# Inverse attention denominators: broadcast by DMA through DRAM instead of by matmul, and denominators in four column groups

## The chip, the cores and the metric

One Trainium2 chip; the same program runs on its 8 cores, each on its own share of the data (4 of 32 sequences), with no traffic between cores. The metric is the device time in microseconds of the slowest core. A core has TensorE (PE, matmuls), VectorE (DVE), ScalarE (ACT), GpSimd (POOL), SyncE (SP, which here issues nearly all DMAs, in order) and 16 DMA engines.

## The reference

For x of shape (32, 2048, 1024), one transformer layer with linear attention (16 heads of 64) and a quantized feed-forward net:

```
Qf, Kf = relu(heads(LN(x) Wq') P) + 1e-6, relu(heads(LN(x) Wk') P) + 1e-6
KV    = sum over tokens of Kf^T V          (per sequence and head, 64x64)
Ksum  = sum over tokens of Kf              (per sequence and head, 64)
denom = Qf . Ksum + 1e-6                   (per token and head)
out   = (Qf KV) / denom
x     = x + LN(out Wo' + bo)
h     = round(256 (LN(x) w1 + b1)) / 256;  h = piecewise-linear GELU(h), rounded
x     = x + LN(round(256 (h w2 + b2)) / 256)
```

## The kernel before

Everything lies in one straight-line program. `p.T`, `p.V`, `p.S`, `p.G` and `p.dma("Y", ...)` append an instruction to the list of TensorE, VectorE, ScalarE, GpSimd and SyncE, with the tokens it waits for; each engine runs its own list strictly in the order in which the Python code appended it. So the order of the calls is the schedule, and a DMA that waits on SyncE holds every later DMA of SyncE.

Phase 1 (`for t in range(NT)`, 64 tiles of 128 tokens, 16 per sequence): layer norm, DMA transpose into `xnT`, projections to K features, V and Q features, and the accumulation of KV and Ksum. Q features go to DRAM (`qscr`), four tiles at a time, with a lag of three tiles. At each sequence's end `kv_mask` makes `ksz[s]`, the Ksum vector spread over a 128 x 8 x 16 matrix that is zero except where column = head, and `m_chunk` folds KV with Wo into `mscr` in DRAM. `k_const` makes the constants `chs` that complete the denominators.

Phase 2 (`for g in range(NBLK * NQ + LAG)`, 32 blocks of 256 tokens, 8 slots i = 0..7 each): in slot (j, i) TensorE does the slot's eighth of the feed-forward net of block j (`ff_w1`, 32 matmuls of 256 columns, and `ff_w2`, 16 matmuls of 512 columns for the slot three before), and between them the "front" of the next block J = j + 1: `fr_den` (denominators), `fr_bc` and `fr_qn` (normalising the Q features `qf`), `fr_o` (attention output by `msb`, twice 16 matmuls), then `fr_sq`, `fr_x2`, `fr_sq2`, `fr_xn` and a DMA transpose into `xnF` for the next block's `ff_w1`. The "fi_" steps end the block before (drain, layer norm, residual, store).

Before the change block J's denominators are one group of 8 matmuls onto 16 PSUM partitions (slot 0, L538); VectorE adds `chs`, takes the reciprocal and splits it into two bf16 halves `hilo` (L541 to L547); in slot 1 eight matmuls with the 0/1 matrix `sel` spread the 16 rows over the 128 partitions of each chunk (`fr_bc`, L554), and `fr_qn` (L564) multiplies `qf` by what stands in PSUM. Block 0's front and the last six Q chunks (`last_q`) stand between the two phases (L870 to L925). The edges of the phases' order that matter:

```
        kv_acc(NT - 1); kv_out(s); last_q(2); fr_den(0); last_q(3)
        for k in range(2): fr_bc(0, k); fr_qn(0, k)
        last_q(4)
        ...
        o_seed(0, 0); fr_o(0, 0); fr_sq(0, 0); kv_mask(s); last_q(6)
```

## Time and profile before

| | |
|---|---|
| times of three runs | 3126.4, 2863.38, 3311.34 us (median 3126.4) |
| the profiled execution's own time | 2864.24 us |
| its span (core 3, the slowest) | 2862.7 us, cores 2856.7 to 2862.7 us |
| mean granted TensorE clock of that core | 0.994 |
| PE, DVE, ACT, POOL busy | 98%, 72%, 64%, 16% |
| mean DMA rate | 171 GB/s |

The span is the time from the first to the last instruction of a core; the profiled execution's own time is 1.5 us more than its span. The profile was taken with the granted clock near full on every core, and its time agrees with the lowest of the three runs. "Idle before" is time in which an engine had nothing under way, with what released it. PE busy is a modelled number: a matmul's record lasts about 160 ns longer than its turn in a stream, so costs of matmuls in a stream are read from the distance between starts.

### The profile page before, as it was taken

What the parts mean: (1) busy time and instruction counts of PE and PEld (TensorE: products, weight loads), DVE (VectorE), ACT (ScalarE), POOL (GpSimd) and SP (SyncE); (2) the same over time, 40 slices, a digit from 0 to 9 for tenths busy, and PEclk for the clock granted to TensorE, in tenths of its full rate; (3) what the DMA queues carried; (4) which work ended last, traced back from release to release, by engine and by line L of the source; (5) the groups of instructions that cost most, each with busy time, mean ns of one, the idle gap of its engine ahead of it and who ended that gap; (6) DMA issues with size and microseconds to landing.
All of it is one profiled execution on the core that took longest, in us unless ns stands there. A gap on an engine that the chain in (4) does not pass through costs nothing.

```text
span 2862.7 us, 47693 instructions; the slowest of 8 cores (2856.7 to 2862.7 us)
## 1 busy us (share of the span) xinstructions
PE 2801.9 (98%) x17762; PEld 1704.7 (60%) x17762; DVE 2063.2 (72%) x2657; ACT 1846.1 (64%) x2953; POOL 467.6 (16%) x1092
## 2 busy tenths in 40 slices
PE   6999999999889999999999999999999999999998
PEld 3444444444456666666666666666666666666665
DVE  5454344443378888788888888788888888878887
ACT  3222222222377787878777787878777788878776
POOL 0111111110001111211111111211111112212111
PEclk8999999999999999999999999999999999999999
DMA  8547999853445555565666556556665655555654
GB/s 261 137 102 130 156 146 160 157 125 85 150 142 177 177 177 174 178 196 184 189 193 182 177 177 197 178 174 182 185 201 180 198 185 163 178 177 179 192 181 147
DMA packets 287618, 488.91 MB, mean 171 GB/s; under 512 B 141424, under 2 KB 174320, under 8 KB 287392
## 3 DMA queue, kind: packets, MB, share of 16 engines
q1 hardware_dynamic: 278176, 469.08, 55.9%
q0 software_dynamic: 9216, 16.78, 5.2%
q8 instruction: 147, 2.41, 0.3%
q14 instruction: 79, 0.65, 0.1%
HBM read 412.90 MB, written 67.11 MB: 168 GB/s over the span
## 4 chain that ended last, share of the span: by engine, by line
PE 96%; DMA 1%; DVE 1%; ACT 1%; issue 0%; POOL 0%; SPq 0%; POOLq 0%; DVEq 0%; ACTq 0%
PE bk L668 31%; PE bk L726 30%; PE bk L371 8%; PE bk L585 8%; PE bk L389 8%; PE bk L402 7%; PE bk L538 1%; PE bk L421 1%; PE bk L554 1%; DMA wkf<-wk_n 1%; PE bk L479 0%; DMA qf<-qscr 0%; PE bk L311 0%; DMA xnF<-xn 0%; ACT stq L226 0%
## 5 line engine op out<-in xcount | busy, mean ns | idle before, releaser
L668 PE MATMUL bk<-xnF,w 128*128 128x256 bf16 x8192 | 937.2, 273 | 4.5 <-DMA xnF<-xn 1.3
L726 PE MATMUL bk<-w2r,yb 128*128 128x512 bf16 x4096 | 925.6, 379 | 0.0
L668 PEld LDWEIGHTS bk<-xnF,w 128*128 128x128 bf16 x8192 | 801.6, 98 | 146.5 <-issue 6.7
L681 ACT ACTIVATE kbuf<-bk,b1s 128x256 int32<-128x256 f32 x1024 | 426.5, 472 | 413.0 <-PE bk L668 413.0
L726 PEld LDWEIGHTS bk<-w2r,yb 128*128 128x128 bf16 x4096 | 398.3, 98 | 441.8 <-issue 6.5
L703 DVE TENSOR_TENSOR y1b<-y1b,y0b 128x1024 f32<-128x1024 f32 x256 | 312.4, 1220 | 152.5 <-ACT y1b L694 151.6
L394 ACT CAST vt<-bk 128x512 bf16<-128x512 f32 x128 | 75.1, 587 | 381.3 <-PE bk L389 381.3
L707 DVE TENSOR_TENSOR jbi<-jbi,y1b 128x1024 f32<-128x1024 int32 x256 | 313.5, 1225 | 8.8
L711 DVE SCALAR_TENSOR_TENSOR jbi<-jbi,y0b 128x1024 f32<-128x1024 f32 x256 | 313.0, 1223 | 5.5
L687 ACT ACTIVATE segb<-kbuf,cst 128x1024 int32<-128x1024 int32 x256 | 295.4, 1154 | 7.6 <-ACT kbuf L681 0.3
L694 ACT ACTIVATE y1b<-segb,cst 128x1024 f32<-128x1024 int32 x256 | 291.4, 1138 | 0.0
L692 ACT ACTIVATE y0b<-segb 128x1024 f32<-128x1024 int32 x256 | 270.1, 1055 | 12.1 <-ACT segb L687 0.4
L376 DVE TENSOR_TENSOR kf<-bk,bkb 128x512 bf16<-128x512 f32 x128 | 88.5, 692 | 228.3 <-PE bk L371 228.3
L371 PE MATMUL bk<-wkp,xnT 128*128 128x512 bf16 x1024 | 233.8, 382 | 2.5 <-DVE xnT L291 1.0
L585 PE MATMUL bk<-msb,qf 128*128 128x512 bf16 x1024 | 231.4, 379 | 2.3 <-ACT bk L573 2.3
L389 PE MATMUL bk<-wv,xnT 128*128 128x512 bf16 x1024 | 231.5, 379 | 2.2 <-DVE wv L225 2.2
L402 PE MATMUL bk<-xnT,wqp 128*128 128x512 bf16 x1024 | 231.8, 379 | 0.8 <-ACT wqp L318 0.8
L612 DVE SCALAR_TENSOR_TENSOR xr<-bk,st,xr 128x512 f32<-128x512 f32 x128 | 90.2, 747 | 148.3 <-POOL st L604 138.4
L716 DVE TENSOR_SCALAR yb<-jbi 128x1024 bf16<-128x1024 f32 x256 | 177.8, 695 | 20.8 <-PE bk L726 0.5
L698 DVE TENSOR_SCALAR jbi<-kbuf 128x1024 int32<-128x1024 int32 x256 | 177.7, 694 | 14.4 <-ACT kbuf L681 5.3
L750 POOL TENSOR_TENSOR st<-st 128x1 f32<-128x1 f32 x64 | 12.3, 193 | 1075.2 <-DVE rr L738 1075.2
L407 ACT ACTIVATE qst<-bk,bqn 128x512 bf16<-128x512 f32 x128 | 88.2, 689 | 148.2 <-PE bk L402 148.2
(110 smaller groups left out, 2313.9 us busy)
## 6 DMA issues: line engine op xcount, KB each, us to landing
w2r<-w2scr SPq DMA_DIRECT2D x512, 512.0 KB, 4.9
xr<-xin SPq DMA_DIRECT2D x128, 512.0 KB, 8.8
yout<-rr SPq DMA_DIRECT2D x64, 512.0 KB, 3.6
qscr<-qst SPq DMA_DIRECT2D x128, 128.0 KB, 6.0
qf<-qscr SPq DMA_DIRECT2D x32, 512.0 KB, 7.4
w<-w_d POOLq DMA_DIRECT2D x32, 256.0 KB, 7.1
mscr<-mst SPq DMA_DIRECT2D x32, 256.0 KB, 4.4
w2scr<-w_d POOLq DMA_DIRECT2D x32, 256.0 KB, 8.4
```

The costliest lines, as they stand in the source:

```text
L371: tt = p.T(lambda e, d=d, hf=hf: e.matmul(bk[hf], lhsT=xnT[(t // 4) % 2][:, d, (t % 4) * 128:(t % 4) * 128 + 128], rhs=wkp[:, d * D + hf * ...
L389: tt = p.T(lambda e, d=d, hf=hf: e.matmul(bk[2 + hf], lhsT=xnT[(t // 4) % 2][:, d, (t % 4) * 128:(t % 4) * 128 + 128], rhs=wv[:, d * D + h ...
L402: tt = p.T(lambda e, d=d: e.matmul(bk[bi], lhsT=wqp[:, d * D + c * 128:d * D + c * 128 + 128], rhs=xnT[b % 2][:, d, :], start=(d == 0), st ...
L585: tt = p.T(lambda e, c=c, b=b, hf=hf: e.matmul(b, lhsT=qf[J % 2][:, c, s2 * 128:s2 * 128 + 128], rhs=msb[:, c * D + hf * 512:c * D + hf * ...
L668: tt = p.T(lambda e, d=d, fc=fc, sub=sub: e.matmul(HB[a][:, sub * 256:sub * 256 + 256], lhsT=w1[:, d * FF + fc * 128:d * FF + fc * 128 + 1 ...
L681: t_k[(g, a)] = p.S(lambda s, sub=sub, fc=fc, o=o: s.activation(out=kbuf[g % 2][:, o:o + 256], in_=HB[a][:, sub * 256:sub * 256 + 256], fu ...
L687: t_seg[g] = p.S(lambda s: s.activation(out=segb, in_=kbuf[g % 2], func=AF.Identity, scale=1.0 / 64.0, bias=c_seg), t_k[(g, 1)], t_y1.get( ...
L694: t_y1[g] = p.S(lambda s: s.activation(out=y1b, in_=segb, func=AF.Gelu, scale=0.25, bias=c_q), t_p.get(g - 1))
L703: t_d[g] = p.V(lambda v: v.tensor_tensor(out=y1b, in0=y1b, in1=y0b[g % 2], op=ALU.subtract), t_y1[g])
L707: t_p[g] = p.V(lambda v: v.tensor_tensor(out=jbf, in0=jbi, in1=y1b, op=ALU.mult), t_d[g], t_j[g])
L711: t_z[g] = p.V(lambda v: v.scalar_tensor_tensor(out=jbf, in0=jbf, scalar=1.0 / 64.0, in1=y0b[g % 2], op0=ALU.mult, op1=ALU.add), t_p[g])
L726: tt = p.T(lambda e, f=f, pr=pr, n=n, s2=s2, hf=hf: e.matmul(ACC[n], lhsT=yb[q % 3][:, f * 256 + s2 * 128:f * 256 + s2 * 128 + 128], rhs=w ...
```

## The change

Block J's denominators are computed in slot 6 of block J - 2 (one block earlier than their use, before in slot 0 of block J - 1). Chunk c goes to column group c % 4: output partitions 32 (c % 4) to +16, with the mask `msk16` changed so that the two heads of chunk c stand in rows c // 4 and 2 + c // 4 of their group. ScalarE first writes the constant `chs` into that PSUM bank (`fr_dseed`), and the matmuls add to it. VectorE takes one reciprocal of 128 x 256 (`fr_rec`, slot 7), SyncE stores it to DRAM (`fr_rstore`), and `rd_load` reads rows of 4 KB back, each broadcast to 64 partitions, in two halves (slots 0 and 1). `fr_qn` takes its factor from `rdb` in SBUF. The matmuls of `fr_bc`, the matrix `sel` and the steps that made `hilo` are gone. Moved: `load_q` from the end of slot 5 to slot 3, the loads of x from the head of slot 7 to its end, `fi_norm(last, 1)` from 5 to 6, `fi_add`/`fi_store(last, 1)` from 6 to 7; `bot` is loaded and centred early in phase 1; block 0's denominators are made in tile 62, its factors in tile 63; the last Q chunks stand in another order; `fr_t` uses other PSUM banks; some buffers lie elsewhere.

```diff
+    rscr = nc.dram_tensor("rscr", [NBLK, 32, 4, 256], F32).ap()
...
-              for i, k in enumerate((176.25, 164))]
+              for i, k in enumerate((144, 164))]
...
-        xn2 = sb("xn2", 144, D, BF16)
-        rden = sb("rden", 146, 256, F32)
-        hilo = sb("hilo", 147, 256, BF16)
+        xn2 = sb("xn2", 148, D, BF16)
+        rden = sb("rden", 150, 256, F32)
+        rdb, rdb0 = (sb(n, k, 4 * 256, F32).rearrange("p (c j) -> p c j", j=256)
+                     for n, k in (("rdb", 152), ("rdb0", 136)))
         yb = [sb(f"yb{i}", k, D, BF16) for i, k in enumerate((184.25, 186.25, 188.5))]
 
-        sel = sb("sel", 198.5, D, BF16)
-        bot = sb("bot", 152, D, F32)
+        bot = sb("bot", 198.5, D, F32)
...
-        t_z = p.V(lambda v: v.memset(sel, 0.0))
+        t_chs = p.V(lambda v: v.memset(chs, 1.0))
...
-        t_sel = p.dma("Y", "c2", sel[0:48], sel_d, t_z)
+        t_bo = p.dma("Y", "c2", bot, bo_d.to_broadcast([128, D]))
...
         def k_const(s, free):
             for c in range(8):
-                tt = p.T(lambda e, c=c: e.matmul(bk[4][0:16, 0:1], lhsT=ksz[s][:, c, :],
-                                                 rhs=one[:, 0:1], start=(c == 0), stop=(c == 7)),
+                q = 32 * (c % 4)
+                tt = p.T(lambda e, c=c, q=q: e.matmul(bk[4][q:q + 16, 0:1], lhsT=ksz[s][:, c, :],
+                                                      rhs=one[:, 0:1], start=(c < 4), stop=(c >= 4)),
                          *((t_ks[s], free) if c == 0 else ()), sig=(c == 7))
-            t_ch[s] = p.V(lambda v: v.tensor_scalar(
-                out=chs[0:16, s:s + 1], in0=bk[4][0:16, 0:1], scalar1=EPS_ATT, scalar2=EPS_ATT,
-                op0=ALU.mult, op1=ALU.add), tt)
+            for q in range(0, 128, 32):
+                t_ch[s] = p.V(lambda v, q=q: v.tensor_scalar(
+                    out=chs[q:q + 16, s:s + 1], in0=bk[4][q:q + 16, 0:1], scalar1=EPS_ATT,
+                    scalar2=EPS_ATT, op0=ALU.mult, op1=ALU.add), tt, t_chs)
             return t_ch[s]
 
...
         def load_q(J):
-            w = t_o[(J - 2, 1)] if J >= 2 else (t_ka[(NT - 1, 1)], t_kv.get(NT - 1))[J]
+            w = t_o[(J - 2, 1)] if J >= 2 else (t_tp[NT - 1], t_kv.get(NT - 1))[J]
             n = 8 * (J // 2)
-            t_qf[J] = p.dma("Y", f"f{J % 2}", qf[J % 2], qscr[J], w, *(t_qs[n + c] for c in range(4, 8)))
+            t_qf[J] = p.dma("Y", f"f{J % 2}", qf[J % 2], qscr[J], w, t_tp[NT - 2], *(t_qs[n + c] for c in range(4, 8)))
...
+
+        def fr_dseed(J):
+            c = chs[:, J // 8:J // 8 + 1].to_broadcast([128, 256])
+            f_free[0] = [p.S(lambda s: s.copy(out=FB[0][:, 0:256], in_=c), *f_free[0], t_ch[J // 8],
+                             own=False)]
+
         def fr_den(J):
             s = J // 8
+            b = FB[0] if J else bk[4]
+            w = f_free[0] if J else [t_ch[BCORE - 2]]
             for c in range(8):
-                tt = p.T(lambda e, c=c: e.matmul(FB[0][0:16, 0:256], lhsT=ksz[s][:, c, :],
-                                                 rhs=qf[J % 2][:, c, :], start=(c == 0), stop=(c == 7)),
-                         *((t_qf[J], t_ks[s], *f_free[0]) if c == 0 else ()), sig=(c == 7))
-            a = p.V(lambda v: v.tensor_scalar(out=rden[0:16], in0=FB[0][0:16, 0:256],
-                                              scalar1=chs[0:16, s:s + 1], scalar2=None, op0=ALU.add),
-                    tt, t_ch[s], t_hl.get(J - 1), t_zero)
-            f_free[0] = [a]
-            b = p.V(lambda v: v.reciprocal(out=rden[0:16], in_=rden[0:16]), a)
-            h = p.V(lambda v: v.tensor_copy(out=hilo[0:16], in_=rden[0:16]), b, t_bc.get(J - 1))
-            t_hl[J] = p.V(lambda v: v.tensor_tensor(out=hilo[32:48], in0=rden[0:16], in1=hilo[0:16],
-                                                    op=ALU.subtract), h)
-
-        def fr_bc(J, k):
-            f = (k + 1) % 2
-            for i in range(2):
-                c = 2 * k + i
-                tt = p.T(lambda e, c=c, i=i: e.matmul(
-                    FB[f][:, i * 256:i * 256 + 256], lhsT=sel[:, c * 128:c * 128 + 128],
-                    rhs=hilo, start=(i == 0), stop=(i == 1)),
-                    *((t_hl[J], t_sel, *f_free[f]) if i == 0 else ()), sig=(i == 1))
-            t_bc[J] = tt
-            t_bc[(J, k)] = tt
+                q = 32 * (c % 4)
+                tt = p.T(lambda e, c=c, q=q: e.matmul(
+                    b[q:q + 16, 0:256], lhsT=ksz[s][:, c, :], rhs=qf[J % 2][:, c, :],
+                    start=(J == 0 and c < 4), stop=(c >= 4), skip_group_check=True),
+                    *((t_qf[J], t_ks[s], *w) if c == 0 else ()), sig=(c == 7))
+            t_dn[J] = tt
+
+        def fr_rec(J):
+            a, b = None, FB[0]
+            if J == 0:
+                a = p.V(lambda v: v.tensor_scalar(out=rden, in0=bk[4][:, 0:256], scalar1=chs[:, 0:1],
+                                                  scalar2=None, op0=ALU.add), t_dn[J], t_ch[0], t_qmm[14])
+                t_dn0.append(a)
+                b = rden
+            t_rc[J] = p.V(lambda v: v.reciprocal(out=rden, in_=b[:, 0:256]), t_dn[J], a, t_rs2.get(J - 1))
+            if J:
+                f_free[0] = [t_rc[J]]
+
+        def fr_rstore(J):
+            t_rs2[J] = p.dma("Y", "rs", rscr[J].rearrange("q j n -> j q n"), rden, t_rc[J])
+
+
+        def rd_load(J, k):
+            dst = rdb if J or k == 0 else rdb0
+            w = t_qn.get(J if k else J - 1) if J else None
+            for hh in range(2):
+                src = rscr[J, 2 * hh + k:2 * hh + k + 1]
+                t_rd[(J, k)] = p.dma("Y", f"rb{k}", dst[64 * hh:64 * hh + 64],
+                                     src.to_broadcast([64, 4, 256]), t_rs2[J], w, t_qmm[14],
+                                     t_xn[NT - 2])
 
         def fr_qn(J, k):
-            f = (k + 1) % 2
             a = qf[J % 2][:, 2 * k:2 * k + 2, :]
+            r = rdb if J or k < 2 else rdb0
             t_qn[J] = p.V(lambda v: v.scalar_tensor_tensor(
-                out=a, in0=a, scalar=EPS_ATT, in1=chunks(FB[f], 2), op0=ALU.add, op1=ALU.mult),
-                t_bc[(J, k)])
-            f_free[f] = [t_qn[J]]
+                out=a, in0=a, scalar=EPS_ATT, in1=r[:, 2 * (k % 2):2 * (k % 2) + 2, :], op0=ALU.add,
+                op1=ALU.mult), t_rd[(J, k // 2)], t_dn[J])
...
         def fr_t(J, s2):
-            b = FB[s2].bitcast(BF16)
+            b = HB[s2].bitcast(BF16)
             for c in range(8):
                 tt = p.T(lambda e, c=c: e.transpose(b[:, c * 128:c * 128 + 128],
                                                     in_=xn2[:, c * 128:c * 128 + 128], identity=idb),
-                         *((t_xa[(J, s2)], *f_free[s2]) if c == 0 else ()), sig=(c == 7))
+                         *((t_xa[(J, s2)], *t_kve[BCORE - 1]) if c == 0 else ()), sig=(c == 7))
...
@@ -802,8 +819,8 @@
                 k_proj(t)
                 k_floor(t)
             if t == NT - 1:
-                t_bo = centre_bo(p.dma("Y", "c4", bot, bo_d.to_broadcast([128, D]), t_qmm[14]))
-                load_q(0)
+                rd_load(0, 0)
+                rd_load(0, 1)
                 for k in range(4):
                     load_m(0, k)
             v_proj(t)
@@ -812,6 +829,7 @@
                 for hf in range(2):
                     t_fq = fold("q", hf, stq, wqp, (0, 1, 2, 3), t_wqc, "VS")
             if t == 6:
+                t_bo = centre_bo(t_bo)
                 t_b1s = p.V(lambda v: v.tensor_scalar(out=b1s, in0=b1s, scalar1=256.0, scalar2=None,
                                                       op0=ALU.mult), t_c1)
             if t == 3:
@@ -845,6 +863,17 @@
                 ln_evac(t + 2)
             elif t + 2 < NT:
                 ln_transpose_dma(t + 2)
+            if t == NT - 3:
+                load_q(0)
+            if t == NT - 2:
+                fr_den(0)
+                fr_rec(0)
+                fr_rstore(0)
+                load_x2(0)
+                load_x2(1)
+            if t == NT - 1:
+                for k in range(4):
+                    fr_qn(0, k)
             if s >= 0 and u == 0:
                 kv_out(s)
             if s >= 0 and 3 <= u < 11:
@@ -868,40 +897,32 @@
             q_store(n + c)
 
         f_free[:] = [list(t_free[2]), list(t_free[3])]
-        t_zero = p.V(lambda v: v.memset(hilo, 0.0), t_tp[NT - 1])
-        load_x2(0)
-        load_x2(1)
+        kv_acc(NT - 1)
+        kv_out(s)
+        t_mb[2] = t_mb[3] = t_qn[0]
+        last_q(2)
+        load_q(1)
         for k in range(4):
             load_w2(k, t_ve[NT - 1])
-        kv_acc(NT - 1)
-        kv_out(s)
-        last_q(2)
-        fr_den(0)
-        last_q(3)
-        for k in range(2):
-            fr_bc(0, k)
-            fr_qn(0, k)
-        last_q(4)
-        for k in range(2, 4):
-            fr_bc(0, k)
-            fr_qn(0, k)
-        last_q(5)
         o_seed(0, 0)
         fr_o(0, 0)
         fr_sq(0, 0)
         kv_mask(s)
-        last_q(6)
+        last_q(3)
+        last_q(4)
         fr_x2(0, 0)
+        o_seed(0, 1)
         fr_sq2(0, 0)
-        last_q(7)
-        t_kte[s] = kv_transpose(s, t_ch[s - 1])
-        k_const(s, t_kte[s])
-        o_seed(0, 1)
+        last_q(5)
         fr_o(0, 1)
         fr_sq(0, 1)
+        last_q(6)
+        t_kte[s] = kv_transpose(s, t_dn0[0])
+        k_const(s, t_kte[s])
         fr_x2(0, 1)
         fr_sq2(0, 1)
         fr_xn(0, 0)
+        last_q(7)
         t_free[4] = [t_ch[s]]
         t_free[5] = t_kve[s]
         for c in range(4):
@@ -920,7 +941,6 @@
         t_b2 = p.dma("Y", "c3", b2t, b2_d.to_broadcast([128, D]), t_qmm[15])
         for n in range(4, 6):
             load_w2(n, t_lastm, *t_mend, t_mk[s], t_qe[127])
-        load_q(1)
         load_x2(2, *t_mend)
         load_x2(3, *t_mend)
 
@@ -929,9 +949,9 @@
             J = j + 1
             front = J < NBLK
             last = j - 1 if j >= 1 else None
-            if front and i == 7 and J + 1 < NBLK:
-                load_x2(2 * J + 2)
-                load_x2(2 * J + 3)
+            if J + 1 < NBLK and i == 7:
+                fr_rec(J + 1)
+                fr_rstore(J + 1)
             if front and i == 4:
                 fr_x2(J, 0)
             if g < NBLK * NQ:
@@ -942,6 +962,8 @@
             if i == (3 if j else 2) and j < NBLK:
                 for n in range(4):
                     acc_seed(j, n)
+            if g == 0:
+                fr_dseed(1)
             if g < NBLK * NQ:
                 ff_k(g, 0)
             if last is not None and i == 3:
@@ -950,7 +972,7 @@
                 fi_stat(last, 1)
             if front and i == 5:
                 fr_sq(J, 1)
-            if last is not None and i == 5:
+            if last is not None and i == 6:
                 fi_norm(last, 1)
             if g < NBLK * NQ:
                 ff_k(g, 1)
@@ -960,18 +982,17 @@
                 ff_seg(g)
             if front and i == 2:
                 o_seed(J, 0)
-            if front and i == 1:
-                fr_bc(J, 0)
-                fr_bc(J, 1)
+            if J + 1 < NBLK and i == 6:
+                fr_dseed(J + 1)
             if front and i == 3:
                 fr_o(J, 0)
+            if front and i == 1 and j:
+                fr_qn(J, 0)
+                fr_qn(J, 1)
             if 1 <= g <= NBLK * NQ:
                 ff_d(g - 1)
             if 1 <= g <= NBLK * NQ:
                 ff_p(g - 1)
-            if front and i == 1:
-                fr_qn(J, 0)
-                fr_qn(J, 1)
             if front and i == 5:
                 fr_xn(J, 0)
                 fr_t_dma(J, 0)
@@ -982,7 +1003,7 @@
             if last is not None and i == 5:
                 fi_add(last, 0)
                 fi_store(last, 0)
-            if last is not None and i == 6:
+            if last is not None and i == 7:
                 fi_add(last, 1)
                 fi_store(last, 1)
             if 1 <= g <= NBLK * NQ:
@@ -990,8 +1011,20 @@
                 ff_y(g - 1)
             if g < NBLK * NQ:
                 ff_j(g)
-            if front and i == 0:
-                fr_den(J)
+            if g == 0:
+                fr_den(1)
+                fr_rec(1)
+                fr_rstore(1)
+            if front and i == (0 if j else 1):
+                rd_load(J, 0)
+            if front and g == 1:
+                fr_qn(J, 0)
+                fr_qn(J, 1)
+            if front and i == (1 if j else 2):
+                rd_load(J, 1)
+            if front and i == 2:
+                fr_qn(J, 2)
+                fr_qn(J, 3)
             if i >= 5 and (J + 1) % 8 == 0 and J + 1 < NBLK:
                 load_m((J + 1) // 8, i - 5)
             if i == 0 and J % 8 == 0 and J < NBLK:
@@ -1005,10 +1038,11 @@
                 if q % NQ == NQ - 1:
                     for n in range(4):
                         fi_drain(q // NQ, n)
-            if front and i == 1:
-                for k in (2, 3):
-                    fr_bc(J, k)
-                    fr_qn(J, k)
+            if J + 1 < NBLK and i == 6:
+                fr_den(J + 1)
+            if J + 1 < NBLK and i == 7:
+                load_x2(2 * J + 2)
+                load_x2(2 * J + 3)
             if front and i == 3:
                 fr_sq(J, 0)
             if front and i == 4:
@@ -1018,8 +1052,8 @@
                 fi_norm(last, 0)
             if front and i == 5:
                 fr_sq2(J, 1)
-                if J + 1 < NBLK:
-                    load_q(J + 1)
+            if front and i == 3 and J + 1 < NBLK:
+                load_q(J + 1)
         for s2 in range(2):
             fi_stat(NBLK - 1, s2)
             fi_norm(NBLK - 1, s2)
@@ -1066,17 +1100,13 @@
     pbd = np.zeros((128, 128), f32)
     pbd[0:64, 0:64] = P_.T
     pbd[64:128, 64:128] = P_.T
-    sel = np.zeros((48, D), f32)
-    for h in range(16):
-        sel[h, h * 64:h * 64 + 64] = 1.0
-        sel[32 + h, h * 64:h * 64 + 64] = 1.0
     mskb = np.zeros((128, 128), f32)
     mskb[0:64, 0:64] = 1.0
     mskb[64:128, 64:128] = 1.0
     msk16 = np.zeros((128, 8, 16), f32)
     for c in range(8):
-        msk16[0:64, c, 2 * c] = 1.0
-        msk16[64:128, c, 2 * c + 1] = 1.0
+        msk16[0:64, c, c // 4] = 1.0
+        msk16[64:128, c, 2 + c // 4] = 1.0
```

## Rows read from the trace of the kernel before

**Rows 1.** The page: busy time of each engine.

```profile
PE 2801.9 (98%) x17762; PEld 1704.7 (60%) x17762; DVE 2063.2 (72%) x2657; ACT 1846.1 (64%) x2953; POOL 467.6 (16%) x1092
```

**Rows 2.** Windows: steady stretch, one block, passage between the phases.

```profile
core 3: us, PE busy (x) PEld busy (x) DVE busy (x) ACT busy (x) POOL busy (x), PEclk, DMA share, GB/s
830.00:2830.00 2000.00, 1997.74 (x13412) 1305.03 (x13410) 1668.61 (x1979) 1587.53 (x2541) 357.80 (x861) 1.00 0.59 182
1300.00:1364.43 64.43, 64.43 (x434) 42.04 (x432) 53.87 (x65) 51.14 (x83) 11.64 (x28) 1.00 0.57 182
...
745.00:850.00 105.00, 82.91 (x528) 50.46 (x526) 64.89 (x86) 62.30 (x109) 9.89 (x28) 0.95 0.50 154
```

**Rows 3.** Groups by line on PE (busy, mean ns, idle before).

```profile
L554 PE MATMUL bk<-hilo,sel 128*128 128x256 bf16 x256 | 38.6, 272 | 3.0 <-DVE hilo L547 1.5 <-DVE qf L564 1.4
L538 PE MATMUL bk<-qf,ksz 128*16 128x256 bf16 x256 | 34.1, 277 | 7.8 <-DMA qf<-qscr 7.8
...
L462 PE MATMUL bk<-one,ksz 128*16 128x1 bf16 x32 | 1.4, 164 | 0.9 <-DVE kvT L458 0.9
```

**Rows 4.** Timeline of PE in one block (start us, us, line, shapes).

```profile
1305.64 1.04 PE L538 MATMUL bk<-qf,ksz 128*16 128x256 bf16 x8
1306.61 3.63 PE L726 MATMUL bk<-w2r,yb 128*128 128x512 bf16 x16
...
1313.57 0.60 PE L554 MATMUL bk<-hilo,sel 128*128 128x256 bf16 x4
1314.01 3.62 PE L726 MATMUL bk<-w2r,yb 128*128 128x512 bf16 x16
...
1328.34 3.62 PE L585 MATMUL bk<-msb,qf 128*128 128x512 bf16 x16
...
1359.54 3.66 PE L668 MATMUL bk<-xnF,w 128*128 128x256 bf16 x32
```

**Rows 5.** Timeline of DVE in the same block.

```profile
1308.84 0.47 DVE L541 TENSOR_SCALAR rden<-bk,chs 16x256 f32<-16x256 f32 x1
...
1311.88 1.23 DVE L703 TENSOR_TENSOR y1b<-y1b,y0b 128x1024 f32<-128x1024 f32 x1
...
1323.76 0.69 DVE L698 TENSOR_SCALAR jbi<-kbuf 128x1024 int32<-128x1024 int32 x1
```

**Rows 6.** Groups by line on DVE: the reciprocal.

```profile
L545 DVE RECIPROCAL rden<-rden 16x256 f32<-16x256 f32 x32 | 55.7, 1741 | 1.1
```

**Rows 7.** Timeline of ACT in slots 5 and 6 of that block.

```profile
1349.46 1.26 ACT L764 ACTIVATE rr<-rr,st 128x1024 f32<-128x1024 f32 x1
...
1355.57 1.55 ACT L681 ACTIVATE kbuf<-bk,b1s 128x256 int32<-128x256 f32 x4
1357.16 1.15 ACT L687 ACTIVATE segb<-kbuf,cst 128x1024 int32<-128x1024 int32 x1
```

**Rows 8.** Window over slot 0 of that block (columns as above).

```profile
1302.00:1310.00 8.00, 8.00 (x58) 5.24 (x56) 7.62 (x10) 5.96 (x8) 0.00 (x0) 1.00 0.99 333
```

**Rows 9.** DMA issues by line: count, KB each, median us to landing.

```profile
xr<-xin SPq DMA_DIRECT2D x128, 512.0 KB, 8.8
...
qscr<-qst SPq DMA_DIRECT2D x128, 128.0 KB, 6.0
qf<-qscr SPq DMA_DIRECT2D x32, 512.0 KB, 7.4
...
bot<-bo_d SPq DMA_DIRECT2D x1, 512.0 KB, 4.1
```

**Rows 10.** Timeline of PE in the passage (idle before, releaser in brackets).

```profile
756.56 3.61 PE L585 MATMUL bk<-msb,qf 128*128 128x512 bf16 x16 [1.42 <-ACT bk L573]
...
783.13 3.65 PE L668 MATMUL bk<-xnF,w 128*128 128x256 bf16 x32 [1.21 <-DVE xnF L651]
794.61 1.86 PE L538 MATMUL bk<-qf,ksz 128*16 128x256 bf16 x8 [7.83 <-DMA qf<-qscr]
...
811.78 3.62 PE L585 MATMUL bk<-msb,qf 128*128 128x512 bf16 x16
```

14 lines of the change are left out of this document (6 added, 8 removed).

## Prediction

> **What bounds the kernel now.** First the busy shares [rows 1]: PE is busy 98% of the span, DVE 72%, ACT 64%. An average hides stages, so next the windows [rows 2]: from 830 to 2830 us PE is busy 1997.7 of 2000 us at a granted clock of 1.00 (2.4 GHz), DVE 83% and ACT 79%. One block takes 64.43 us, all PE. The reader is to see that in phase 2 every instruction taken from TensorE's stream shortens the block by its turn, as long as nothing else comes last. Between the phases, 745 to 850 us, PE is idle for 22 of 105 us: there waits decide. DMA engines are 57% busy over a block, but 99% in slot 0 [rows 8].
>
> A matmul's record overlaps the next, so I take turns from starts [rows 4]. Eight `fr_den` matmuls take 1306.61 - 1305.64 = 0.97 us, four `fr_bc` matmuls 1314.01 - 1313.57 = 0.44 us. The busy figure of L554, 38.6 us [rows 3], counts each group's tail, which already overlaps the next matmul; its turns come to less.
>
> **Term 1, the broadcast matmuls go.** Eight per block, 2 x 0.44 = 0.88 us, with nothing beside them on PE. In the blocks J = 2 to 31, whose front lies in the steady stretch, 30 x 0.88 = 26.4 us. (Blocks 0 and 1 are in the passage term.)
>
> **Term 2, denominators in four groups.** The count stays 8 matmuls of 256 columns per block. Upper end: they take 0.97 us as now, gain 0. Lower end: if groups that write different partitions run side by side, two rounds of 0.11 us, plus a start of some 0.1 us (0.97 - 8 x 0.109) and the spacing of starts: about 0.36 us. The trace shows no two matmuls side by side, so this is my choice: the eight one-column matmuls of `k_const`, with the same 16 columns of weights, take 1.4 / 4 = 0.35 us a group with a record of 0.164 us [rows 3], so starts can be (0.35 - 0.164) / 7 = 27 ns apart. Fetching weights is not what spaces `fr_den` by 109 ns; the 256 columns streaming through one place are, and the new layout has four places. I take 0.36: 30 x (0.97 - 0.36) = 18.3 us; the other end is rival 1.
>
> The Trainium skill, TensorEngine Tiling (Array Packing), section Tiling Modes, says that tiles work independently, loading weights and multiplying in parallel, and that a change of tiling mode drains the engine. No row shows the first; 0.1 us of start would agree with the second. By its first statement alone term 2 is the 18 us above, without it zero. TensorE: Matmul & The Clock Gate, Part 3, gives 2.38 times for three column tiles; by that figure the estimate is 0.97 / 2.38 = 0.41 us, 17 us in all.
>
> **Term 3, a new wait on PE: the seed.** `fr_den` of slot 6 now adds to what `fr_dseed` wrote, so PE waits for ACT. PE gets there when slot 6's `ff_w2` ends, 1359.54 in the block shown [rows 4]. ACT: in slot 6 it now has `fi_norm(last, 1)` as well, and the seed comes last. From the start of the four L681 activations at 1355.57 to L687 are 1.59 us, `fi_norm` takes about 1.15 of its recorded 1.26, L687 about 1.05 of 1.15, the seed of 256 columns some 0.42 like one L681 with its tail [rows 7]: 1355.57 + 1.5 + 1.15 + 1.05 + 0.42 = 1359.7, less up to 0.2 because slot 5 is rid of its `fi_norm`. So PE waits between 0 (ACT early by 0.2) and 0.6 us (both activations at full recorded length); I take 0.15 us, 30 x 0.15 = 4.5 us lost, 0 to 18. Behind the wait on PE stands slot 7's `ff_w1`, which starts later by the wait and by no more.
>
> **Term 4, DVE and the two round trips in a steady block: 0.** DVE loses L541, L546 and L547; one reciprocal stays, 1.74 us whether 16 or 128 partitions, as its 256 columns are the same [rows 6], and moves to the head of slot 7. `fr_qn` reads its factor from SBUF instead of PSUM; same shape, I take no change. DVE gets about 3.0 - 1.7 = 1.3 us per block and is no bound. The new wait is at the head of slot 1: `fr_qn(J, 0)` stands before `ff_d`, and all of DVE queues behind it if the factors are not there. DVE reaches it at 1308.84 + 1.77 = 1310.6 (end of slot 0, where L541 began [rows 5], plus the moved reciprocal). The load goes out at about 1302, the start of slot 0, behind 1 MB of w2 and 1 MB of x that used to go earlier. With its own 0.5 MB that is 2.5 MB at the 333 GB/s of a full slot [rows 8], 7.5 us, plus issue: landed at about 1310. The x loads, in the same crowd, land after 8.8 us, a 4 KB row broadcast to 128 partitions (`bot`) after 4.1 [rows 9]; so 1306 to 1311. What may it cost? From 1308.84 to the end of L698 in slot 2 are 15.5 us [rows 5]; less 3.0 of removed steps 12.5, so with no wait DVE has the last `fr_qn` done at 1323.1, and PE wants it for `fr_o` at 1328.34 - 0.88 = 1327.5 [rows 4]. Some 4.4 us of lateness are covered; a landing after 1315 costs its excess each block. The second half is issued when the first is used and has a slot to land. The store has from slot 7 to slot 0, some 6 us, against 6.0 us for the 128 KB stores to `qscr` [rows 9]; were it late, SyncE would hold the load, then slot 0's w2 loads, whose buffers are wanted three slots later. The loads of q, x and the fi_ stores moved by one or two slots keep over two slots to land; `fi_add` moved to slot 7 is used in the next block. `load_q` in slot 3 waits for an `fr_o` of the block before, long past.
>
> The Trainium skill, DMA: Bandwidth & Descriptors, section on why a DMA increments its semaphore by 16, speaks against the store: the number of engines used divides the slowest dimension of both sides, and here that is 4 in DRAM, so 4 of 16 engines would carry it. No row shows such a shape. In a steady block 4.4 us of cover would take it; in the passage it would add to both round trips.
>
> **Term 5, the passage.** Two chains. (a) Before `fr_o(0, 0)`, at 756.56 [rows 10]. Now the denominators of block 0 are made in tile 62, a q load after the last transpose has landed, so PE may wait there some 2 us for it; then reciprocal (1.8 plus an add 0.5), a store (6.0), 1 MB of factors (issue 1.5, 4 to 9 us to land), and 2 MB of `msb` behind them on SyncE. I get 753 to 758 for `fr_o(0, 0)`, say 755.5. From there to the first `ff_w1` are 26.6 us; the new order seeds `fr_o(0, 1)` right after `fr_x2(0, 0)` and leaves some 2.5 us less. First `ff_w1` at 779.5, 3.6 earlier. (b) From the first `ff_w1` to `fr_o(1, 0)` are 811.78 - 783.13 = 28.65 us, with 7.8 us of waiting for `qf` [rows 10]; `load_q(1)` now goes out long before. The new chain: `ff_w1` and `fr_den` 4.0, reciprocal 1.8, store 5, load 0.7 + 4.1, `fr_qn` 1.3, second load 4.8, `fr_qn` 1.3: 23 us. Gain 5.6. Together 9; from -4 (each DMA at the 8.8 of a crowded time) to +20 (idle time of 22 us nearly gone).
>
> The rest is nothing: the `sel` memset and load go, a 512 KB `bot` load comes ahead of the wq loads in phase 1, `k_const` has four small DVE steps for one, three times.
>
> **Sum.** Against the profiled execution, 2864.2: - 26.4 - 18.3 + 4.5 - 9 = 2815.0. The median of the three runs, 3126.4, lies far off the lowest, 2863.4, with which the profile agrees; my number stands beside the latter.
>
> **Rivals.** (1) The four groups run one after the other: term 2 is 0, 2833. For it: the trace has no overlap anywhere. Against: the 27 ns spacing. (2) The waits are kinder: the seed costs nothing and the passage gives 16: 2864.2 - 26.4 - 18.3 - 16 = 2803.5. For it: 22 us of idle time; against: two more round trips through DRAM in its chains. (3) Slower: the factors for slot 1 land late in every block, because slots 7 and 0 are the ones where the DMA engines are full and x and w2 stand ahead. It decides from a landing after 1315 on; at 1320 (the load held by a late store and another 2 MB of neighbours' traffic) each block costs 5 us, 30 x 5 = 150: 2965. It takes a landing 18 us after issue, where the x loads take 8.8. It is slower by over 2% from a stall of 3.6 us a block on. (4) The change doesn't do what it says: PE's turns go but DVE or ACT (83 and 79% busy) becomes the bound, blocks stay near 64 us, 2850 to 2864. Against: both lose or gain under 1.5 us of over 10 us idle per block.
>
> **Chances.** Forecast 0.55, (1) 0.2, (2) 0.17, (3) 0.05, (4) 0.03. The measurement of this kernel can tell about 2% from no change, 57 us. Faster by over 2% means under 2807: (2) and the low edge of the forecast, 0.2. Slower by over 2%: 0.05. Within: 0.75. The range: bottom 2798 from rival (2) with a passage of 20, top 2840 from rival (1) with a passage worth 2.
>
> **What would show it.** Right: no L554; a block of 64.43 - 0.88 - 0.61 + 0.15 = 63.1 us; `fr_den` to the next matmul under 0.5 us with its eight starts in two bunches; PE idle before `fr_den` of at most 0.2 us for ACT; PE idle in the passage about 10 us, not 22. Wrong: PE idle before `fr_o` for DVE `fr_qn`, with DVE waiting in slot 1 for `rdb`; a passage in which PE waits for the store or for `msb`.

## The result

The changed kernel is slower. Its runs take 2980.1 and 2981.5 us, those of before 2863.2 to 2865.7 us: a ratio of 1.040, 95% interval 1.037 to 1.043. The medians over all runs, 3046.8 and 2864.8 us, hold runs in which one die was at a lower clock than the other; such runs are left out of every comparison here, and experiment 8's profiled execution was one. The profiled execution took 2981.5 us with a span of 2980.0; before it was 2864.2. The forecast was 2815, with a range of 2798 to 2840.

The page of the profile after, busy time by engine, the chain that ended last by line, and the DMA issues of the factors:

```profile
PE 2806.8 (94%) x17506; PEld 1675.3 (56%) x17506; DVE 2024.4 (68%) x2573; ACT 1856.2 (62%) x2984; POOL 525.0 (18%) x1092
...
DMA rdb<-rscr 11%; PE bk L743 10%; PE bk L603 9%; PE bk L685 8%; PE bk L402 7%; PE bk L371 7%; PE bk L389 7%; DVE jbi L728 5%; DVE y1b L720 4%; DVE jbi L724 4%; SPq L88 3%; DVE yb L733 3%; DVE qf L583 3%; DVE rr L787 2%; DVE rden L563 2%
...
rdb<-rscr SPq DMA_DIRECT2D x128, 256.0 KB, 6.1
```

PE ran 256 instructions fewer than in [rows 1] and was busy 5 us more, in a span 117 us longer. The longest entry of the chain is now a transfer, the new load of the factors. Groups by line on PE and DVE after (busy, mean ns; idle before, releasers):

```profile
L603 PE MATMUL bk<-msb,qf 128*128 128x512 bf16 x1024 | 271.1, 425 | 103.1 <-DVE qf L583 86.0 <-DMA msb<-mscr 10.2 <-DVE rr L755 6.9
L550 PE MATMUL bk<-qf,ksz 128*16 128x256 bf16 x256 | 12.6, 273 | 1.4 <-ACT bk L541 1.4
L583 DVE SCALAR_TENSOR_TENSOR qf<-qf,rdb 128x512 bf16<-128x512 bf16 x128 | 82.6, 687 | 235.2 <-DMA rdb<-rscr 235.2
```

`fr_den` (L550, before L538) fell from 34.1 to 12.6 us [rows 3], L554 is gone, and the seed (L541) costs PE 1.4 us in all. But `fr_o` (L603) waits 86.0 us for `fr_qn` (L583), and `fr_qn` waits 235.2 us for its factors. Windows over the same stretches as [rows 2] (columns as there):

```profile
830.00:2830.00 2000.00, 1893.69 (x12410) 1201.96 (x12407) 1537.54 (x1780) 1506.53 (x2431) 390.08 (x822) 0.98 0.66 190
...
745.00:850.00 105.00, 80.32 (x511) 47.67 (x510) 57.08 (x78) 60.35 (x107) 9.19 (x28) 0.92 0.58 161
```

In the steady stretch PE is idle for 106.3 us where it was idle for 2.3, at a granted clock of 0.98 instead of 1.00.

**Where the 117 us are.** I split the span at two matmul groups, `fr_o(1, 0)` and `fr_o(31, 0)`. The first starts at 816.22 (before 811.78 [rows 10]): +4.4. From it to the second are 2048.4 us against 1935.6 (2864.63 and 2747.35 less the starts above): +112.8. From there to the end both need 115.4. Removed turns should have given 30 x (0.88 + 0.64) = 45.6 us, so 45.6 + 112.8 = 158.4 us were lost in thirty steady blocks, 5.3 in each.

One of these blocks, timeline of PE after. It answers to [rows 4]:

```profile
1329.12 0.39 PE L550 MATMUL bk<-qf,ksz 128*16 128x256 bf16 x8
1329.45 3.67 PE L685 MATMUL bk<-xnF,w 128*128 128x256 bf16 x32
...
1336.40 3.66 PE L685 MATMUL bk<-xnF,w 128*128 128x256 bf16 x32
...
1357.24 3.66 PE L685 MATMUL bk<-xnF,w 128*128 128x256 bf16 x32
1363.68 5.30 PE L603 MATMUL bk<-msb,qf 128*128 128x512 bf16 x16 [2.78 <-DVE qf L583]
1368.82 3.62 PE L743 MATMUL bk<-w2r,yb 128*128 128x512 bf16 x16
```

Slot 0 begins at 1336.40. `ff_w1` of slot 3 ends its turn at 1357.24 + 3.50 = 1360.74, and `fr_o` starts 2.9 us later. Then its sixteen matmuls take 1368.82 - 1363.68 = 5.14 us, not 3.45. A window over them shows a granted clock of 0.68, against 1.00 over the sixteen of `fr_o(J, 1)` of the block before:

```profile
1363.50:1368.80 5.30, 5.12 (x16) 1.99 (x17) 5.23 (x11) 4.64 (x10) 0.97 (x4) 0.68 0.00 0
1311.50:1315.10 3.60, 3.60 (x19) 1.58 (x18) 0.00 (x0) 3.60 (x5) 1.27 (x5) 1.00 0.37 50
```

So part of the stretch ran at 1.2 GHz instead of 2.4. The wait costs itself and 1.7 us more: 62.9 + 2.9 + 1.7 = 67.5 of the block's 67.6 us (1396.71 less 1329.12). Over the whole steady stretch it is the same: 106.3 us idle in 2000 / 68.28 = 29.3 blocks are 3.6 each, and the rest of the 5.3 is slower matmuls.

DVE after, in the same block (start, us, in brackets the idle time before):

```profile
1331.20 1.75 DVE L563 RECIPROCAL rden<-bk 128x256 f32<-128x256 f32 x1
...
1343.51 0.69 DVE L715 TENSOR_SCALAR jbi<-kbuf 128x1024 int32<-128x1024 int32 x1
1350.54 1.29 DVE L583 SCALAR_TENSOR_TENSOR qf<-qf,rdb 128x512 bf16<-128x512 bf16 x2 [6.34 <-DMA rdb<-rscr]
...
1362.11 1.29 DVE L583 SCALAR_TENSOR_TENSOR qf<-qf,rdb 128x512 bf16<-128x512 bf16 x2
```

DVE stands still for 6.3 us at the head of slot 1 with slot 1's and slot 2's work behind the waiting `fr_qn`. It finishes the last `fr_qn` at 1363.40, 12.85 us after the landing at 1350.54. PE wants it 1360.74 - 1336.40 = 24.35 us after slot 0 begins. So a landing up to 24.35 - 12.85 = 11.5 us after slot 0 begins is free; this one came after 14.1. SyncE's queue in that stretch, and the entry of the chain of waits behind it:

```profile
1333.03 0.60 SPq L88 DMA_DIRECT2D rscr<-rden  x1
1336.50 0.34 SPq L88 DMA_DIRECT2D yout<-rr  x1
1336.93 1.49 SPq L88 DMA_DIRECT2D w2r<-w2scr  x2
1338.47 0.90 SPq L88 DMA_DIRECT2D xr<-xin  x2
1339.47 1.39 SPq L88 DMA_DIRECT2D rdb<-rscr  x2
1343.59 0.88 SPq L88 DMA_DIRECT2D w2r<-w2scr  x2
```

```profile
1340.23 10.29 DMA rdb<-rscr
```

The load is two DMAs of 256 KB. Its issue begins 3.1 us into slot 0: the moved `fi_store` waits until DVE's L787 is done, then four issues of w2 and x take 2.4 us. The half lands 10.3 us after the first of the two issues is complete, while a window over 1340.3 to 1350.5 shows the DMA engines full at 317 GB/s. The landing comes 2.6 us later than the free 11.5, and the other steady blocks are alike: the landing comes 12.8 to 20.1 us after slot 0 begins (median 14.7), and PE waits between 1.4 and 3.7 us in each. The store of the reciprocals is not what holds the load: over the whole run SyncE waits for it four times, 8.5 us together.

The passage, timeline of PE after, to be held against [rows 10]:

```profile
736.49 0.40 PE L550 MATMUL bk<-qf,ksz 128*16 128x256 bf16 x8
...
760.23 5.32 PE L603 MATMUL bk<-msb,qf 128*128 128x512 bf16 x16 [10.21 <-DMA msb<-mscr]
765.39 5.34 PE L402 MATMUL bk<-xnT,wqp 128*128 128x512 bf16 x24
...
774.02 1.89 PE L402 MATMUL bk<-xnT,wqp 128*128 128x512 bf16 x8
...
777.37 1.90 PE L402 MATMUL bk<-xnT,wqp 128*128 128x512 bf16 x8
...
790.97 5.32 PE L685 MATMUL bk<-xnF,w 128*128 128x256 bf16 x32 [2.81 <-DVE xnF L669]
...
816.22 3.61 PE L603 MATMUL bk<-msb,qf 128*128 128x512 bf16 x16 [2.66 <-DVE qf L583]
```

Before, the only Q-projection matmuls (L402) between `fr_o(0, 0)` and the first `ff_w1` were these:

```profile
760.01 3.62 PE L402 MATMUL bk<-xnT,wqp 128*128 128x512 bf16 x16
```

The passage differs from core to core, so one core's number says little. `fr_o(1, 0)` starts between 807.4 and 813.5 us on the eight cores before, mean 811.3, and between 806.8 and 818.7 after, mean 811.3 again. The 4.4 us are those of the slowest core; on the mean of the cores the passage is neither shorter nor longer.

### The profile page after: what moved, and what is told of

Read it like the earlier page. It is cut to its first block, busy times and chain, and to the rows that moved or that the text cites. A ratio compares the mean times of both kernels' runs of the same rounds, so it can differ in the third digit from the quotient of the medians.

```text
span 2980.0 us, 47351 instructions; the slowest of 8 cores (2948.9 to 2980.0 us)
## 1 busy us (share of the span) xinstructions
PE 2806.8 (94%) x17506; PEld 1675.3 (56%) x17506; DVE 2024.4 (68%) x2573; ACT 1856.2 (62%) x2984; POOL 525.0 (18%) x1092
## 4 chain that ended last, share of the span: by engine, by line
PE 49%; DVE 26%; DMA 14%; issue 4%; SPq 4%; ACT 2%; POOL 1%; DVEq 0%; POOLq 0%; ACTq 0%
DMA rdb<-rscr 11%; PE bk L743 10%; PE bk L603 9%; PE bk L685 8%; PE bk L402 7%; PE bk L371 7%; PE bk L389 7%; DVE jbi L728 5%; DVE y1b L720 4%; DVE jbi L724 4%; SPq L88 3%; DVE yb L733 3%; DVE qf L583 3%; DVE rr L787 2%; DVE rden L563 2%
## 5 line engine op out<-in xcount | busy, mean ns | idle before, releaser
L603 PE MATMUL bk<-msb,qf 128*128 128x512 bf16 x1024 | 271.1, 425 | 103.1 <-DVE qf L583 86.0
L603 PEld LDWEIGHTS bk<-msb,qf 128*128 128x128 bf16 x1024 | 107.7, 107 | 254.7 <-issue 164.4
L583 DVE SCALAR_TENSOR_TENSOR qf<-qf,rdb 128x512 bf16<-128x512 bf16 x128 | 82.6, 687 | 235.2 <-DMA rdb<-rscr 235.2
L767 POOL TENSOR_TENSOR st<-st 128x1 f32<-128x1 f32 x64 | 12.4, 193 | 1257.1 <-DVE rr L755 1257.1
L402 PE MATMUL bk<-xnT,wqp 128*128 128x512 bf16 x1024 | 231.7, 379 | 0.8 <-ACT wqp L318 0.8
```

Source lines behind the costliest of these rows:

```text
L402: tt = p.T(lambda e, d=d: e.matmul(bk[bi], lhsT=wqp[:, d * D + c * 128:d * D + c * 128 + 128], rhs=xnT[b % 2][:, d, :], start=(d == 0), st ...
L603: tt = p.T(lambda e, c=c, b=b, hf=hf: e.matmul(b, lhsT=qf[J % 2][:, c, s2 * 128:s2 * 128 + 128], rhs=msb[:, c * D + hf * 512:c * D + hf * ...
```

## The experiments

The theory after the trace: the blocks are lost because the first half of the factors lands some 2.6 us too late for `fr_qn`, which stands ahead of everything else that DVE does in slots 1 and 2. Rivals: 64 partitions reading the same 4 KB row of DRAM is slow in itself; `fr_den` in four groups, or the seed, costs something that the trace hides; other moved steps (`fi_norm`, x) take DVE or SyncE time. All ratios are to runs of the kernel before on the same chip.

**1. The wait moved on DVE, the load left where it is.**

```diff
-            if front and i == 1 and j:
-                fr_qn(J, 0)
-                fr_qn(J, 1)
             if 1 <= g <= NBLK * NQ:
                 ff_d(g - 1)
...
-            if front and g == 1:
+            if front and i == 1:
                 fr_qn(J, 0)
                 fr_qn(J, 1)
```

> The one edit: in slot 1 the first two fr_qn stand behind ff_j instead of ahead of ff_d, so that VectorE's own slot-1 work no longer queues behind the wait for the factors. Theory A (the cost is where VectorE waits: 6.3 us idle in slot 1, then 12.8 us of work to the last fr_qn, so PE waits 2.8 to 3.7 us at fr_o and the matmuls after it run 1.7 us longer at a lower granted clock): the factors land at the same time, 14 us after slot 0 begins, but VectorE has 5.2 us of work for the wait, PE's wait at fr_o goes, a block takes 63.0 us instead of 68.3, and the time is 2981 - 30 x 5.3 = 2822, at most 2835. Theory B (the second half of the factors, issued later now, becomes late instead): fr_qn of the second half waits, a block stays over 66 us, 2920 or more.

2846.7 to 2850.3 us, ratio 0.994 [0.992, 0.996]. DVE's and PE's timelines of a block whose slot 0 begins at 1301.38:

```profile
1317.25 1.29 DVE L583 SCALAR_TENSOR_TENSOR qf<-qf,rdb 128x512 bf16<-128x512 bf16 x2 [2.66 <-DMA rdb<-rscr]
```

```profile
1325.71 3.62 PE L603 MATMUL bk<-msb,qf 128*128 128x512 bf16 x15
```

The factors land 15.9 us after slot 0 begins, later than in the changed kernel, and `fr_o` waits for nothing, since DVE has done slot 1's work first. One moved step takes back some 130 us. The load is no faster than it was; what cost the time was that work stood behind the wait. The 2822 expected was missed by 25 us and more: the thirty steady blocks take 1917.7 us where 1890 were expected. Most take 62.97 to 63.5, but the three with a new `msb` take 66.4 to 66.9, and the blocks after them 64.7 to 65.6.

**2. The load moved, the wait left where it is.** The first half goes out in slot 7, ahead of slot 0's w2 and of x.

```diff
-            if front and i == (0 if j else 1):
+            if front and g == 1:
                 rd_load(J, 0)
+            if J + 1 < NBLK and i == 7:
+                rd_load(J + 1, 0)
```

> The one edit: the first half of the factors is loaded in slot 7, ahead of that slot's w2 loads and the x loads, instead of in slot 0 behind them. Theory A (the load is late because 2 MB of w2 and x stand ahead of it on queues that are full): it lands 4 to 7 us after its issue, VectorE does not wait in slot 1, a block takes 63.0 us, the time is about 2822. Theory B (the load is slow of itself, because 64 partitions read one and the same row of DRAM): it still takes about 10 us from issue to landing; issued 3 us earlier, it would be 3 us less late, and the time would be 2825 to 2860, with VectorE still waiting some 3 us.

2848.5 to 2850.8 us and one run of 2876.6; ratio 0.996 [0.991, 1.000]. SyncE's queue, slot 0 beginning at 1300.37, and the group of `fr_o`:

```profile
1301.08 1.13 SPq L88 DMA_DIRECT2D rdb<-rscr  x2
1302.30 1.01 SPq L88 DMA_DIRECT2D w2r<-w2scr  x2
1303.36 2.57 SPq L88 DMA_DIRECT2D xr<-xin  x2
```

```profile
L603 PE MATMUL bk<-msb,qf 128*128 128x512 bf16 x992 | 239.4, 391 | 38.3 <-DVE rr L755 18.2 <-DVE qf L583 9.6 <-DMA msb<-mscr 8.7
```

The load's issue begins 2.4 us earlier than in the changed kernel, counted from slot 0's begin; it has landed at 1308.78, 8.4 us after that begin instead of 14.1, and the steady wait is gone too. The theory is shown from both sides: the late landing and the work behind the wait are both needed for the loss, and mending either takes back some 130 of the 158 us. The 2822 expected was missed again, by 26 us and more: the three blocks with a new `msb` take 66.7, 69.0 and 71.9 us.

**3. The bytes ahead: x loads back at the head of slot 7**, with `fi_norm` and `fi_add` of the last block back in their slots.

```diff
             if J + 1 < NBLK and i == 7:
+                load_x2(2 * J + 2)
+                load_x2(2 * J + 3)
                 fr_rec(J + 1)
                 fr_rstore(J + 1)
...
-            if last is not None and i == 6:
+            if last is not None and i == 5:
                 fi_norm(last, 1)
...
-            if last is not None and i == 7:
+            if last is not None and i == 6:
                 fi_add(last, 1)
                 fi_store(last, 1)
```

> The edit: the two x loads back at the head of slot 7, with fi_norm(last, 1) and fi_add(last, 1) back in slots 5 and 6, as before the change. Theory A (queue ahead): 1 MB less ahead of the factors, which is 3 us of the full rate of 333 GB/s; they land 11 instead of 14 us after slot 0 begins, PE's wait at fr_o falls from 3.3 us to below 0.5, 2981 - 30 x 4.5 = 2846, with fi_norm back in slot 5 perhaps 3 us less. Theory B (slow of itself): the landing moves by the 0.9 us of issue time on SyncE alone, PE's wait to 2.4 us, 2950 or so.

2898.4 to 2912.9 us, ratio 1.014 [1.007, 1.020]: half way. PE, DVE and SyncE in a block:

```profile
1315.48 3.66 PE L685 MATMUL bk<-xnF,w 128*128 128x256 bf16 x32
...
1340.98 3.61 PE L603 MATMUL bk<-msb,qf 128*128 128x512 bf16 x15 [1.00 <-DVE qf L583]
```

```profile
1327.86 1.29 DVE L583 SCALAR_TENSOR_TENSOR qf<-qf,rdb 128x512 bf16<-128x512 bf16 x2 [4.40 <-DMA rdb<-rscr]
```

```profile
1313.29 0.60 SPq L88 DMA_DIRECT2D rscr<-rden  x1
1315.72 1.04 SPq L88 DMA_DIRECT2D w2r<-w2scr  x2
1321.67 1.12 SPq L88 DMA_DIRECT2D rdb<-rscr  x2
```

```profile
1313.29 8.31 DMA rscr<-rden
```

The load lands 5.6 us after issue instead of 10.3. But x now stands ahead of the store too, which takes 8.3 us, and SyncE issues the load, which needs the store, only 6.2 us into slot 0. Over the run SyncE waits 188.5 us for the store, where in the changed kernel it was 8.5. So neither theory's time came: one delay went and another took part of its place. Landing 12.4 us after slot 0 begins, less the 11.5 that are free: 0.9, and PE waited 1.0. The `fr_o` after it runs 3.45 us, at a clock of 1.00: this wait cost no more than itself.

**4. Other rows.** Each of the 64 partitions reads a row of its own, out of x; the amount of data is the same. The reciprocals are thus not used.

```diff
-                src = rscr[J, 2 * hh + k:2 * hh + k + 1]
-                ... src.to_broadcast([64, 4, 256]) ...
+                r = 64 * (2 * hh + k)
+                src = xin[J // 8, 256 * (J % 8) + r:256 * (J % 8) + r + 64, :]
+                ... src.rearrange("p (j n) -> p j n", j=4) ...
```

> Leaves out the use of the stored reciprocals: the same number of bytes goes to the same partitions in the same 4 KB rows, with the same waits, but from 64 different rows of x instead of one row of the stored reciprocals 64 times (the factors are then wrong). Theory A (queue ahead): no change, 2980 within 10, the load takes 10 us from issue to landing in slot 0. Theory B (one DRAM row read 64 times is slow): the load takes 5 us or less, PE's wait at fr_o falls, 2850 or less.

2973.0 to 2984.1 us, ratio 1.040 [1.036, 1.044], as the changed kernel:

```profile
L604 PE MATMUL bk<-msb,qf 128*128 128x512 bf16 x1024 | 274.5, 429 | 105.2 <-DVE qf L584 86.2 <-DMA msb<-mscr 9.9 <-DVE rr L756 9.2
```

86.2 us of waiting against 86.0. Many readers of one DRAM row are no part of the cause.

**5. Experiments 1 and 2 together.**

> Both edits together: the first half of the factors is loaded in slot 7 ahead of w2 and x, and the first two fr_qn stand behind ff_j in slot 1. Each alone left a block at about 63.2 us with single waits of up to 1 us. If lateness of the factors was all that cost time in the steady blocks, nothing is left there: PE's waits for fr_qn go to 0 outside the blocks that also load msb, 2840 us, some 7 less than either alone. If something else limits (an engine near its bound), it stays at 2847.

2848.7 to 2852.5 us, ratio 0.994 [0.992, 0.996]: no better than either. DVE's wait for the load falls on to 71.9 us, but PE's waits for `fr_o` stay at 40: 8.6 for `msb` in the passage, 12.7 in three places behind `fr_qn`, and 18.9 in the three blocks J = 8, 16, 24, where a new `msb` is loaded. A quiet block takes 62.96 us, as expected; what is left is in these places and in the passage, and the 2840 expected was missed by 9 to 13 us.

**6. The column groups undone**, on top of 5: all eight `fr_den` matmuls write the same 16 partitions, so that the denominators of different chunks are summed into one.

```diff
-                q = 32 * (c % 4)
+                q = 0
...
-                    start=(J == 0 and c < 4), stop=(c >= 4), skip_group_check=True),
+                    start=(J == 0 and c == 0), stop=(c == 7), skip_group_check=True),
```

> As the run before, but all eight fr_den matmuls of a block write the same 16 partitions one after the other (the denominators are then wrong, the count, shapes and weights the same). If the four groups run side by side and that alone made fr_den short, its turn on PE goes from 0.33 us back to 0.97, 30 x 0.64 = 19 us more. If the shorter turn came from the seed (start=False) or from the earlier slot, it stays at 0.33 us.

PE in one block:

```profile
1362.33 1.03 PE L550 MATMUL bk<-qf,ksz 128*16 128x256 bf16 x8
1363.30 3.67 PE L685 MATMUL bk<-xnF,w 128*128 128x256 bf16 x32
```

0.97 us for eight, to the hundredth what it was before the change; in four groups it is 0.33. One run, 2863.2 us, is 11 to 15 above those of experiment 5, where the turns alone would give 31 x 0.64 = 20. With a single run the time agrees in sign only; what is shown is the turn, and the block with it: a quiet block takes 63.59 us here and 62.96 in experiment 5, 0.63 more.

**7. The passage mended**, on top of 5: the `bot` load moved from the head of phase 1 to tile 3, block 0's x loads behind the factors and `msb`.

```diff
+                t_bo = p.dma("Y", "c2", bot, bo_d.to_broadcast([128, D]))    # tile 3, was ahead of wq
...
                 fr_rstore(0)
-                load_x2(0)
-                load_x2(1)
...
                 for k in range(4):
                     load_m(0, k)
+                load_x2(0)
+                load_x2(1)
```

> As the run with both edits, and two more: bot is loaded in tile 3 instead of ahead of the wq loads, and between the phases the msb and factor loads go out ahead of the two x loads. The first bears on the fold of wq (PE idle there 2.7 us before, 6.2 after the change): 0 to 3 us less. The second bears on fr_o(0, 0), which waited 8.7 to 10.2 us for msb: 1 MB less ahead at 333 GB/s is 3 us. Together 3 to 6 us less, 2835. If fr_o(0, 0) waits for something else that is as late, nothing.

2843.8 to 2847.4 us, ratio 0.993 [0.991, 0.995]. In the passage `fr_o(0, 0)` starts at 756.90 and still waits 9.5 for `msb`; `fr_o(1, 0)` at 813.08. On the mean of the eight cores these are 753.0 and 809.6, where experiment 5, with the passage as in the changed kernel, had 754.4 and 812.1, and experiment 1, with the same passage, 753.9 and 810.6. So moving the x loads brought 1 to 2.5 us at most, where 3 were expected. On the profiled cores the 5 us by which this run lies below experiment 5 are in the steady stretch (1917.4 us against 1922.6), which the edits do not touch. One of the blocks with a new `msb`, its PE, and the chain of waits:

```profile
2287.34 3.57 PE L602 MATMUL bk<-msb,qf 128*128 128x512 bf16 x8 [8.05 <-DVE rr L754]
```

```profile
2269.78 15.57 DMA rdb<-rscr
```

Here the second half of the factors takes 15.6 us: two of the four 512 KB pieces of `msb`, with w2 and x, went out on SyncE in the ten microseconds before it.

**8. Column groups alone.** The kernel before with `fr_den` and `k_const` in four groups, factors by matmul as they were (32 columns of weights instead of 16, so that high and low halves come out in rows of their own; one more small DVE step).

```diff
-                    FB[0][0:16, 0:256], lhsT=ksz[s][:, c, :], ... start=(c == 0), stop=(c == 7)
+                    FB[0][q:q + 32, 0:256], lhsT=ksz[s][:, c, :], ... start=(c < 4), stop=(c >= 4)
...
+            r = p.V(lambda v: v.tensor_scalar(out=rden, in0=rden, scalar1=m_lo, ...), h)
+            t_hl[J] = p.V(lambda v: v.scalar_tensor_tensor(out=hilo, in0=hib, scalar=m_hl, in1=rden,
+                                                           op0=ALU.mult, op1=ALU.add), r, ...)
```

> The kernel before with one part of the change alone: denominators in four column groups (32 columns of weights, so that each group holds its heads twice), while the factors are still broadcast by matmuls, hi in rows 0 to 15 and lo in rows 16 to 31 of each group. VectorE does one more step per block, 0.3 us, on all 128 partitions. Theory: the groups are worth 0.97 - 0.33 = 0.64 us of PE per block and need no DMA, 2864 - 32 x 0.64 = 2844. Rival: the longer chain on VectorE before fr_bc (2.95 to 3.3 us) or a drain of the array between shapes makes PE wait, 2860 or more.

2850.3, 2850.5 and 2854.3 us, ratio 0.995 [0.993, 0.997]. From its profile I take only the turn, in a stretch at a granted clock of 1.00: 1336.45 to 1336.79, 0.34 us. This part of the change alone is worth 14 us, where its turns alone would give 20; no profile here shows where the other 6 are.

**9. Only the order of the bytes**: the x loads behind the first half of the factors, all else as in the changed kernel.

```diff
-            if J + 1 < NBLK and i == 7:
-                load_x2(2 * J + 2)
-                load_x2(2 * J + 3)
...
                 rd_load(J, 0)
+            if front and i == 0 and j:
+                load_x2(2 * J)
+                load_x2(2 * J + 1)
```

> The changed kernel with one edit: the two x loads of slot 7 go out in slot 0, behind the first half of the factors instead of ahead of it. Nothing else moves. Theory (bytes ahead in the queues): issue 0.9 us earlier and 1 MB less ahead, so the factors land about 4 us earlier, 10 instead of 14 us after slot 0 begins, inside the 11.5 us that VectorE's work allows; PE's wait at fr_o goes in most blocks, 2981 - 30 x 4.5 = 2845. Rival (what makes it late is the w2 traffic and the machine's other cores, not what this kernel put ahead): 1 us earlier at most, 2940 or more.

2868.9 to 2877.2 us, ratio 1.003 [1.002, 1.004]. Most of the loss is gone, not all. In the block whose slot 0 begins at 1307.82, DVE and PE:

```profile
1320.70 1.29 DVE L583 SCALAR_TENSOR_TENSOR qf<-qf,rdb 128x512 bf16<-128x512 bf16 x2 [5.09 <-DMA rdb<-rscr]
```

```profile
1333.82 3.61 PE L603 MATMUL bk<-msb,qf 128*128 128x512 bf16 x15 [1.50 <-DVE qf L583]
```

Landing 12.9 us after slot 0 begins, less 11.5: 1.4, and PE waited 1.5. In this block the load still took 10.0 us from issue, though x was issued behind it (SyncE has `rdb` at 1310.13, `xr` at 1311.34). So the order on SyncE does not keep a load's place when the engines are full. Over the run it did help: in the thirty steady blocks the first half lands 8.7 to 16.9 us after slot 0 begins, median 12.2 where 10 was expected, against a median of 14.7 in the changed kernel, and PE waited 21.9 us for `fr_qn` instead of 86.0. From the begin of the first half's issue to its landing the medians are 11.6 us with x just ahead (changed kernel), 9.3 with x right behind (this one), 7.4 with slot 0's w2 and x both behind (experiment 2, the 22 blocks in which DVE waited for it) and 5.8 with x sent before slot 0 (experiment 3). Bytes behind the load seem to count, then, if less than bytes ahead; but in experiment 3 the load is also issued later, so this reading is argued and not shown.

**10 and 11. `msb` in two slots.** On top of 2 (experiment 10) and of 5 (experiment 11), with the edits of 7: the four pieces of `msb` go out in slots 5 and 6, two each, instead of one each in 5, 6, 7 and 0; and `last_q(3)`, `last_q(4)` stand ahead of `fr_o(0, 0)`.

```diff
-            if i >= 5 and (J + 1) % 8 == 0 and J + 1 < NBLK:
-                load_m((J + 1) // 8, i - 5)
-            if i == 0 and J % 8 == 0 and J < NBLK:
-                load_m(J // 8, 3)
+            if i in (5, 6) and (J + 1) % 8 == 0 and J + 1 < NBLK:
+                load_m((J + 1) // 8, 2 * i - 10)
+                load_m((J + 1) // 8, 2 * i - 9)
```

> First half of the factors in slot 7 ahead of w2 and x (as in the second run), bot in tile 3, msb and factors ahead of x between the phases (as in the seventh), and new: the 2 MB of msb that every eighth block loads in slots 5, 6, 7 and 0 go out in slots 5 and 6, where the DMA engines are less full; last_q(3) and last_q(4) go ahead of fr_o(0, 0), where PE waited 9.5 us for msb. Three blocks lost 4 to 8 us each there, and a lower clock behind it. If the factors are late in those blocks because of msb in slots 7 and 0: 15 to 20 us less than the seventh run, 2828. If not: 2845.

> As the run before, with the first two fr_qn behind ff_j in slot 1 as well. That holds back the issue of the second half by 5 us (it waits for them), but takes VectorE's slot-1 work out of the wait. If the second half is now what comes last, this is slower than the run before by 3 to 10 us; if the first half is, faster.

Experiment 10: 2838.8 and 2840.0 us, ratio 0.991 [0.989, 0.993]. Experiment 11: 2841.1 and 2843.5, too few for an interval. The three blocks' waits are 3.5, 2.5 and 2.3 us in 10 and 5.1, 2.8 and 3.0 in 11, after 4.3, 4.6 and 8.1 in 7. So experiment 10 gained some 6 us on experiment 7, of the 15 to 20 expected. With the load early, a late `fr_qn` brings nothing. The reordered passage was a miss: `fr_o(0, 0)` at 761.68, `fr_o(1, 0)` at 817.87 in 10, and 757.69 and 814.23 in 11, which has the same passage. On the mean of the eight cores `fr_o(1, 0)` is at 814.3 and 812.4, 3 to 5 us later than in 7.

**12. The best version.** Experiment 10 with `last_q` back in its place, and `msb` issued ahead of block 0's factors.

```diff
             if t == NT - 1:
-                rd_load(0, 0)
-                rd_load(0, 1)
                 for k in range(4):
                     load_m(0, k)
+                rd_load(0, 0)
+                rd_load(0, 1)
+                load_x2(0)
+                load_x2(1)
```

> As the run with msb moved to slots 5 and 6, but last_q(3) and last_q(4) back behind fr_o(0, 0) (ahead of it they made it 5 us later, as their stores hold SyncE), and between the phases msb goes out ahead of the first factors, while these are still on their way to DRAM: the 2 MB of msb, which fr_o(0, 0) waited for, are issued some 2 to 5 us earlier. If the passage is set by these two, fr_o(0, 0) starts at 752 to 755 instead of 761.7 and the time is 2839 - 7 to 9 = 2831. If the ACT seeds or the factors come last there, 2834 or more.

2838.7 to 2840.4 us, before 2864.9 to 2871.5; ratio 0.990 [0.989, 0.992]. It beats both kernels. Its steady stretch by windows, then PE's timeline:

```profile
830.00:2800.00 1970.00, 1959.59 (x13180) 1267.50 (x13178) 1634.78 (x1888) 1600.69 (x2575) 401.95 (x864) 1.00 0.70 203
```

```profile
761.02 5.38 PE L602 MATMUL bk<-msb,qf 128*128 128x512 bf16 x16 [13.34 <-DVE kvb L441]
...
816.87 6.46 PE L602 MATMUL bk<-msb,qf 128*128 128x512 bf16 x16 [3.10 <-DVE qf L582]
...
1264.70 3.61 PE L602 MATMUL bk<-msb,qf 128*128 128x512 bf16 x16 [3.25 <-DVE rr L754]
```

PE is idle for 10 of 1970 us. Most blocks take 62.96 or 62.97 us, `fr_o` to `fr_o`; 64.43 before. The passage was missed again: on the mean of the eight cores `fr_o(1, 0)` is at 811.5, 3 us earlier than in 10 and 2 later than in 7, and the 2831 expected was missed by 8 us. The profile puts PE's wait down to L441, but what is late before it on DVE is `fr_qn`, which waits 16.9 us for the factors: the four loads of `rdb`, now issued behind the four of `msb`, take 11.0 to 15.0 us to land, where in the changed kernel they took 4.8 to 7.8 and `msb` up to 11.8. Whichever goes first, the last of this crowd lands at about the same time: `fr_qn` gets its last factors at 759.1 here, `fr_o` its `msb` at 760.2 there.

## Why the prediction was wrong

**Terms 1 and 2: right.** The turns came off as worked out: no L554, and eight `fr_den` take 0.33 us, where I chose 0.36 out of 0.36 to 0.97. Experiment 6 brings back 0.97 by putting the groups on one place, so side by side is shown, and rival 1 is out. The trace thus agrees with the Trainium skill, TensorEngine Tiling (Array Packing), section Tiling Modes, that tiles work independently. Where the Trainium skill, TensorE: Matmul & The Clock Gate, Part 3, has a factor of 2.38 for three column tiles, four here give 0.97 / 0.33 = 2.9. In experiment 12 the sum of both stands in every quiet block: 64.43 - 0.88 - 0.64 = 62.91, measured 62.96.

**Term 3, the seed: mis-sized.** 4.5 us taken, 1.4 measured. In the block shown the seed takes 0.36 us from 1328.61, and PE reaches `fr_den` only at 1329.12.

**Term 4, DVE and the round trips at 0: the step that failed.** Its frame held. I had 12.5 us of DVE's work between landing and `fr_o`; it is 12.85. I had a landing 13 us after slot 0 begins as the last free one; it is 11.5, mostly because the 0.97 us of `fr_den` also leave slot 0 and I subtracted only the 0.88 of the broadcasts. What failed is the sentence "With its own 0.5 MB that is 2.5 MB at the 333 GB/s of a full slot [rows 8], 7.5 us, plus issue: landed at about 1310", 8 us after slot 0 begins. It was 14.1 in the block shown and 14.7 in the median. Three things were wrong in it:
- The issue. I wrote "plus issue" and gave it 0.5 us. `fi_store`, moved ahead of it, waits for DVE; then four issues of 0.4 to 1.0 us each stand ahead, and its own two take 1.4. The first of these is in the queues 3.8 us into slot 0, the second 4.5.
- What comes behind. Slot 1's w2 goes out at 1343.59, into the same queues, before the load has landed. In its 10.2 us of flight the engines moved 10.2 x 317 = 3.2 MB, where I had counted 2.5 MB from slot 0's begin on, with nothing behind. The load did not land ahead of what was issued after it, and in experiment 9, with x behind, one still took 10.0 us. How much of the lateness is due to the bytes behind, and how much to the other cores' traffic, no run separates.
- The comparison with `bot` (4.1 us) was from a quiet time; the x loads beside it (8.8) were the row to take. Issue at 3.8 us plus 8.8 is 12.6, already past 11.5.

Then each microsecond cost more than one: 2.9 us of wait brought 1.7 us at a lower granted clock. I had priced "its excess each block".

**Term 5, the passage: mis-sized, the gain is not there.** 9 us of gain forecast; 4.4 lost on the core shown, 0.0 on the mean of the eight. Of its two bets, (a) `fr_o(0, 0)` by 755.5: it was 760.2 here, but 754.8 on the mean of the cores (754.9 before), and 753.4 to 755.3 in experiments 1, 2, 3, 5 and 9 with the same passage. That part was close. PE waits 9 to 10 us there for `msb`, 2 MB issued behind the factors, a load that I named in the chain and gave no landing time. (b) The ramp: I had 23 us from the first `ff_w1` to `fr_o(1, 0)`; it is 816.22 - 790.97 = 25.3, of 28.65 before, so 3.4 gained of 5.6. What was lost lies between `fr_o(0, 0)` and the first `ff_w1`: 30.7 us, of 26.6 before, where I had forecast 2.5 less (30.4 and 27.0 on the mean of the cores). What failed there is that I left out what the new order of the Q chunks puts into that stretch: 40 matmuls of L402 instead of 16, and 24 more at 3.45 / 16 = 0.216 us are 5.2 us. The lower clock after the wait for `msb` adds 1.7 us in `fr_o(0, 0)`, and idle time gives some of it back.

**The sum again, with measured terms.** 2815.0 - 0.9 (groups) - 4.5 (seed, whose 1.4 us lie in the next term) + 158.4 (blocks) + 13.4 (passage: 9 and 4.4, on the slowest core) = 2981.4; the profiled execution took 2981.5. For experiment 12: 2815.0 - 0.9 - 4.5 + 14.9 + 14.1 = 2838.6, measured 2838.7, where 14.9 is what its thirty blocks lack of the 45.6 us of gain (1904.9 us against 1935.6) and 14.1 the passage (816.87 against 811.78, and the 9). The range had a slip too: rival 2 with a passage of 20 gives 2864.2 - 26.4 - 18.3 - 20 = 2799.5, not 2798.

**The rival that came true** was the third. It named the place (slots 7 and 0 full, x and w2 ahead), the wait, and 2965 us at 5 us a block; it was 5.3. The mechanism was right, but that 5 and 5.3 agree is luck: the 5 was a landing 18 us after slot 0 begins, held by a late store, against a cover of 13. Measured were a landing at 14 to 15, no late store, a cover of 11.5 and the lower clock on top; with the rival's own cover a landing at 14.1 would have cost 1 us a block. I gave it 0.05 because "it takes a landing 18 us after issue". That sentence measured from slot 0's begin and called it issue, and took the x loads' 8.8 us as proof of distance, where 8.8 was counted from their own, later, issue. A margin of 5 us, on a transfer whose nearest rows were 4.1 and 8.8 us, deserved far more chance than that. Rival 4 is out: DVE and ACT do not bound a block of 62.96 us.

**Open.** How to shorten the wait before `fr_o(0, 0)`, which comes between 753.5 and 762.6 us on the profiled core of every kernel but that of experiment 8: experiments 7, 10 and 12 moved it from `msb` to ACT's seed and to the factors, and none took bytes out of that stretch. What makes single cores late in the passage: within one execution of the changed kernel `fr_o(1, 0)` differs by 12 us between cores, before by 6. Whether the store to `rscr`, with 4 rows as its slowest dimension, is carried by few engines: in experiment 3 it took 8.3 us, but x stood ahead of it, and no run separates them.

## What to carry to other kernels

Price a transfer in a full stretch from the moment its own issue ends on its queue, and do not count on its landing ahead of what is issued behind it; the nearest row is that of a load in the same slot, not of the same kind of load in a quiet one. An engine that runs in order must have nothing behind a wait that others need: moving two instructions of DVE behind the slot's own work was worth as much as a landing 6 us earlier, some 130 us of 2980. When work changes its place in a list, count it in the stretch where it now stands. And try the parts of a change apart: the four column groups alone gave 0.5%, the best version, with the load and `msb` moved as well, 1.0%, and the whole as first put cost 4%.

## What the runs showed of the hardware that I had not expected

- Thin matmuls in four groups run side by side, 2.9 times as fast and not four times: eight of 256 columns with 16 columns of weights take 0.33 us, 0.97 on one place. With 32 columns of weights it is 0.34.
- A wait of PE can cost over half as much again. In the changed kernel, after idle times of 2.83 to 3.72 us the next sixteen matmuls took 4.94 us or more by the record; after 1.37 to 2.25 us, 3.61. Between these it went either way: 2.48, 2.65 and 2.78 us were followed by 5.30, and 2.60, 2.66, 2.73 and 2.81 by 3.61.
- A load of 256 KB took 3.3 us from issue at the least (experiments 3, 4 and 10) and up to 19.5 (experiment 2).
- One DRAM row read by 64 partitions is no slower than 64 rows: 86.0 and 86.2 us of waiting.
- The issue of a DMA holds SyncE for different times: two w2 issues took 0.88 us at 1343.59 and 1.49 at 1336.93.
